# Rotary products summed on GpSimd before TensorE's transposes, and projections moved ahead of softmax steps

## The reference

```python
qkv = x @ qkv_w.T + qkv_b            # 32 query heads, 8 key heads, 8 value heads, 64 wide
q = _apply_rope(q, cos, sin)         # [x1*cos - x2*sin, x2*cos + x1*sin]
k = _apply_rope(k, cos, sin)
logits = einsum('bqhmd,bkhd->bhmqk', q, k) / 8      # causal, window 128
e = exp(logits - max);  w = e / (sum(e) + exp(sink - max))
out = einsum('bhmqk,bkhd->bqhmd', w, v) @ out_w.T + out_b
```

## Time and profile before

| what | us |
|---|---|
| median of three runs (2179.29, 2182.62, 2183.5) | 2182.62 |
| the profiled execution, its own time | 2175.44 |
| its span, from the first to the last instruction | 2173.4 |
| TensorE busy in the span | 1990.2 (92%) |
| VectorE busy | 1172.4 (54%) |
| ScalarE busy | 775.8 (36%) |
| GpSimd busy | 614.6 (28%) |

### The profile page before, as it was taken

One profiled execution on the slowest core, in us unless ns is written; L12 is line 12 of the kernel. 1 busy time (PEld: TensorE's weight loads), 2 busy tenths in 40 slices (PEclk: granted clock), 3 DMA queues, 4 the chain that ended last, 5 costly groups with the idle time before them and its releaser, 6 DMA issues. The chain is left out here.

```text
span 2173.4 us, 49370 instructions
## 1 busy us (share of the span) xinstructions
PE 1990.2 (92%) x17680; PEld 1484.0 (68%) x17681; DVE 1172.4 (54%) x2333; ACT 775.8 (36%) x1463; POOL 614.6 (28%) x1100
## 2 busy tenths in 40 slices
PE   4999999999999999997799999999999599999998
PEld 3877787778777877786566666666666355666665
DVE  6566556655665566555566566666666122222221
ACT  3333333333333333333245444445455211211211
POOL 2232223222322232222222333332332310014443
PEclk9999999999999999999799999999999799999999
DMA  4011111111111111111323323323222155222221
GB/s 160 26 50 37 48 36 48 36 48 36 48 36 48 36 48 36 48 33 52 94 57 81 83 59 81 79 63 81 74 68 66 39 173 185 70 66 66 66 64 43
DMA packets 123545, 139.65 MB, mean 64 GB/s; under 512 B 16706, under 2 KB 118086, under 8 KB 121642
## 3 DMA queue, kind: packets, MB, share of 16 engines
q1 hardware_dynamic: 117674, 123.95, 20.3%
q0 software_dynamic: 5760, 14.06, 2.0%
HBM read 85.07 MB, written 53.52 MB: 64 GB/s over the span
## 5 line engine op out<-in xcount | busy, mean ns | idle before, releaser
L1032 ACT ACTIVATE xe<-bankXT 128x512 f32<-128x512 f32 x512 | 289.2, 596 | 324.8 <-PE bankXT L1173 317.8
L1073 DVE TENSOR_REDUCE xmax<-bankX 128x4 f32<-128x1024 f32 x256 | 309.2, 1210 | 133.5 <-PE bankX L1162 133.5
L1162 PE MATMUL bankX<-stk,stq 96*128 96x256 f32 x1024 | 230.7, 311 | 24.0 <-DMA rw<-in_rw 10.2
L543 DVE TENSOR_TENSOR oTl<-bankV,oTh 128x512 fp32r<-128x512 f32 x128 | 88.5, 691 | 303.9 <-ACT oTh L431 303.9
L1173 PE MATMUL bankXT<-stq,stk 98*128 98x256 f32 x1024 | 220.5, 298 | 6.7 <-ACT xe L1032 2.8
L1162 PEld LDWEIGHTS bankX<-stk,stq 96*128 96x128 f32 x1024 | 162.3, 198 | 55.5 <-issue 32.0
L649 PE MATMUL bankQ<-wqh,xnTh 128*128 128x512 f32 x384 | 188.5, 491 | 0.0
L1472 DVE TENSOR_TENSOR hid<-bankU,gate 128x512 f32<-128x512 f32 x72 | 49.8, 691 | 245.0 <-PE bankU L1525 241.9
L1173 PEld LDWEIGHTS bankXT<-stq,stk 98*128 98x128 f32 x1024 | 157.4, 191 | 32.0 <-ACT xe L1032 27.6
L360 POOL TENSOR_TENSOR prob<-prob,rden 128x1024 f32<-128x1024 f32 x64 | 121.9, 1905 | 170.5 <-DVE rden L539 170.5
L1188 PE MATMUL bankN<-xe,cT 128*32 128x256 f32 x2048 | 166.2, 397 | 0.2 <-ACT xe L1032 0.2
(11 more groups left out here) (177 smaller groups left out, 4090.2 us busy)
## 6 DMA issues: line engine op xcount, KB each, us to landing
stackk_d<-chl SPq DMA_DIRECT2D x96, 128.0 KB, 2.3
stackq_d<-q2hl SPq DMA_DIRECT2D x96, 128.0 KB, 2.3
stk<-stackk_d SPq DMA_DIRECT2D x32, 384.0 KB
stq<-stackq_d SPq DMA_DIRECT2D x128, 96.0 KB
wexp<-in_wexp SPq DMA_DIRECT2D x8, 1536.0 KB, 8.5
x_d<-x SPq DMA_DIRECT2D x64, 128.0 KB, 2.0
xin<-xg_d SPq DMA_DIRECT2D x40, 128.5 KB, 2.1
x<-in_x SPq DMA_DIRECT2D x32, 128.0 KB, 2.2
```

Source lines behind the costliest of these rows:

```text
L543: nc.vector.tensor_tensor(oTl[g % 2][:], bV[:, 0, :].rearrange("p (a b) -> p a b", a=4), oTh[g % 2][:].bitcast(F32), ALU.subtract).then_in ...
L1032: nc.scalar.activation(xe[q % 8][:].rearrange("p n m -> p (n m)"), bT[:, q % 2, :], ACT.Exp).then_inc(s_xe, 1)
L1073: nc.vector.tensor_reduce(xmax[tile[1] % 2][:, :, a:b + 1:b - a].rearrange("p m h -> p h m"), bS[:, 2 * (pr % 2):2 * (pr % 2) + 2, :].rear ...
L1162: ins = nc.tensor.matmul(bS[:, q % 4, m * D:(m + 1) * D], stq[p][0:96, hd, m * P:(m + 1) * P], stk[p][0:96, hd // 4, :], start=True, stop= ...
```

## The change

The sum of the two rotary products is formed on GpSimd by a new helper, `rope_sum`, into three new buffers `roped[0..2]`. `turn_qk` then makes four transposes instead of eight. A new semaphore `s_rsum` counts the sums: `turn_qk(n)` waits for sum n, and `rope(c)` waits for sum c-2 (before: for the transposes of c-2). `rope_sum(c)` waits for `rope(c)` and, from c = 3 on, for the transposes that read the same one of the three buffers.

The order changes on all four engines. On TensorE, P2 stands ahead of Q0, P3 ahead of T0, P4 ahead of R0, P5 ahead of O1, and Q3 behind R2. On VectorE, `rope(2)` stands ahead of `shift(u, 1)`, `rope(3)` and `rest_O(u, 0)` ahead of `denominator(u, 1)`, and `rope(4)` right behind it. On ScalarE, `evac_PT(u, 0)` and `evac_qk(1)` stand ahead of `exp_probs(u, 1)`, and `evac_O(u, 2)` ahead of `evac_qk(3)`. On GpSimd the five sums are put between the existing steps, and `rsqrt(0)` moves ahead of the split of `q2`.

```diff
+        roped = [sb(f"roped{p}", [P, 512]) for p in range(3)]
...
+            def rope_sum(tile, c):
+
+                t = num(tile)
+                pool.wait_ge(s_rope, t * 5 + c + 1)
+                need(pool, s_turn, t * 5 + c - 2 if c >= 3 else t * 5)
+                nc.gpsimd.tensor_tensor(roped[c % 3][:], ropeC[c % 2][:], ropeD[c % 2][:], ALU.add).then_inc(s_rsum, 1)
...
                 dve.wait_ge(s_qkv, t * 6 + c + 1)
-                need(dve, s_turn, t * 5 + max(c - 1, 0))
+                need(dve, s_rsum, t * 5 + max(c - 1, 0))
...
-                pe.wait_ge(s_rope, t * 5 + n + 1)
+                pe.wait_ge(s_rsum, t * 5 + n + 1)
                 need(pe, s_qkT, t * 5 + n)
                 for j in range(4):
-                    for i, r in enumerate((ropeC[n % 2], ropeD[n % 2])):
-                        ins = turn(bT[:, 0, j * P:(j + 1) * P], r[:, j * P:(j + 1) * P], i == 0, i == 1)
+                    ins = turn(bT[:, 0, j * P:(j + 1) * P], roped[n % 3][:, j * P:(j + 1) * P])
...
                 if rear:
                     scores(u, 1)
                 if front:
+                    project(tile, 2)
                     turn_qk(tile, 0)
-                    project(tile, 2)
+                    project(tile, 3)
                 if rear:
                     turn_probs(u, 0)
                 if front:
                     turn_qk(tile, 1)
-                    project(tile, 3)
+                    project(tile, 4)
                 if rear:
                     results(u, 0)
                     turn_probs(u, 1)
                 if front:
                     turn_qk(tile, 2)
-                    project(tile, 4)
                 if rear:
                     project_out(u, 0)
                     results(u, 1)
                     turn_probs(u, 2)
                 if front:
-                    turn_qk(tile, 3)
+                    project(tile, 5)
                 if rear:
                     project_out(u, 1)
                     results(u, 2)
                 if front:
-                    project(tile, 5)
+                    turn_qk(tile, 3)
```

More of the change, by code:

```diff
@@ L205, in attention @@
         s_xnTp, s_xnTh, s_xnT = sem("s_xnTp"), sem("s_xnTh"), sem("s_xnT")
-        s_qkv, s_rope, s_v = sem("s_qkv"), sem("s_rope"), sem("s_v")
+        s_qkv, s_rope, s_v, s_rsum = sem("s_qkv"), sem("s_rope"), sem("s_v"), sem("s_rsum")
         s_turn, s_qkT = sem("s_turn"), sem("s_qkT")
@@ L367, in body @@
                     rsqrt(1, v)
+                if front:
+                    rope_sum(tile, 0)
                 if rear:
@@ L370, in body @@
                 if front:
+                    rope_sum(tile, 1)
+                    rope_sum(tile, 2)
                     pool.wait_ge(s_ctx[p], (h + 1) * 16)
                     split(tile, ctx[p][:], chl[p], s_stk[p], s_chl, g_c, 3)
+                    rope_sum(tile, 3)
                 if rear:
                     norm_probs(u, 1)
+                if front:
+                    rope_sum(tile, 4)
+                    if below(num(tile), NT - 2):
+                        rsqrt(0, (h + 1, p))
                 if prep:
@@ L377, in body @@
                     split(v, q2[:], q2hl[p], s_stq[p], s_q2hl, g_q2, 4)
-                if front:
-                    if below(num(tile), NT - 2):
-                        rsqrt(0, (h + 1, p))
             rsqrt(0, (0, 0))
@@ L443, in body @@
                 if rear:
-                    exp_probs(u, 1)
                     evac_PT(u, 0)
@@ L448, in body @@
                 if rear:
+                    exp_probs(u, 1)
                     evac_O(u, 0)
@@ L455, in body @@
                     evac_PT(u, 2)
+                    evac_O(u, 2)
                 if front:
@@ L458, in body @@
                 if rear:
-                    evac_O(u, 2)
                     evac_PT(u, 3)
@@ L585, in body @@
                     rope(tile, 1)
+                    rope(tile, 2)
                 if rear:
@@ L588, in body @@
                 if front:
-                    rope(tile, 2)
+                    rope(tile, 3)
                 if rear:
+                    rest_O(u, 0)
                     denominator(u, 1, soft)
-                    rest_O(u, 0)
                 if front:
-                    rope(tile, 3)
+                    rope(tile, 4)
                 if prep:
@@ L601, in body @@
                     stats1((h + 1, p))
-                if front:
-                    rope(tile, 4)
                 if rear:
```

## The result

| what | before | changed |
|---|---|---|
| median (runs; lowest to highest), us | 2183.06 (4; 2179.29 to 2185.14) | 2160.16 (4; 2151.27 to 2162.8) |
| changed / before, 95% interval | | 0.9896 [0.9875, 0.9917] |
| span of the profiled execution | 2173.4 | 2149.0 |
| mean of the two tiles laid out | 31.06 | 30.57 |
| last residual, the end of the self-attention | 1035.26 | 1019.68 |

The kernel became faster by 22.9 us, where 9 were forecast. The direction was right, and the forecast gain was less than half of what came. The 2160.16 lies inside the range of 2158 to 2187, but at its fast end: to anything faster than 2163 the prediction gave 0.07.

What follows compares the result with a forecast made beforehand. TensorE, busy 92%, sets the pace together with VectorE's chain to GpSimd's normalisation. Per tile 0.51 us saved less 0.18 for the sums, times 31, less about 1 us in the last tile: 9 us, so 2173.6; range 2158 to 2187.

Steps and rivals of the forecast that it cites:

- the two tiles laid out: Consecutive attention tiles from P0 at 511.33 and 542.56: 31.23 and 30.88 us, forecast 30.65 and 30.44 before the sums' cost.
- The gaps: Four new waits of TensorE in a tile, at P3, O0, T2 and O2: 1.0, 0.7, 1.3 and 0.7 us.
- The rival of a longer exclusion: VectorE kept out behind GpSimd's queue after the c = 2 sum: 30 us slower, 2213; all slower cases together 0.12.
- The dear and the cheap sum: Rivals on GpSimd's additions: 1.47 us, total 2186, within slower cases of 0.11; 1.12 us or less, 2163 to 2169, 0.25.
- the 15 us worked out from that page: Total saving if a GpSimd sum takes 1.12 us, in proportion to the skill's 4497 ns for 2048 wide.
- a gain of 0.33: Per attention tile: 0.51 us saved by the new layout less 0.18 lost to the sums on GpSimd.
- the 0.04: Loss per tile at Q1: its sum reaches TensorE at 10.48, TensorE is free at 10.43.
- 0.14: Time TensorE follows the end of GpSimd's normalisation, taken from T0 (520.44 to 520.58) and applied to T2.
- The sentence that closes the layout: Of 2.2 us saved in transposes and 1.6 of old gaps per tile, all but 0.51 goes into four new gaps.
- a loss of 1 us for the last tile: Last tile, without a front: denominator(1) stands behind rest_O(0), so about 1 us is lost.
- tile A: Attention tile beginning with P0 at 511.33, 31.23 us long; forecast to end at 30.65 before the sums' cost.

Runs made afterwards that it cites:

- experiment 10: Experiment 8 with R2 ahead of O1 on TensorE; 2097.85 us, ratio 0.9626 to the kernel before.
- Experiment 4: The changed kernel itself measured and profiled once more, nothing altered; 2158.24 us, ratio 0.9904 to the kernel before.
- experiment 7: Experiment 1 plus, on ScalarE alone, the copies of T0 and Q1 ahead of the exponential of half 1; 2155.31 us, ratio 0.9881 to the kernel before.
- experiment 5: The changed kernel with 36 extra unused matmuls on TensorE behind the last tile's output projection; 2160.91 us, ratio 0.9907 to the kernel before.
- experiment 8: Experiment 3 with each GpSimd normalisation split into two 512-wide halves, each with its own semaphore count; 2125.39 us, ratio 0.9739 to the kernel before.
- experiment 11: Experiment 10 with the second layer norm's statistics behind rope(2) and rsqrt(1) ahead of the sum of c = 3; 2079.71 us, ratio 0.9541 to the kernel before.
- 6: The kernel before with 36 extra unused matmuls on TensorE behind the last tile's output projection; 2181.98 us, ratio 1.0005 to the kernel before.
- 9: The changed kernel with 67 extra matmuls ahead of its first tile to delay its start; 2171.85 us, ratio 0.9969 to the kernel before.
- experiment 3: The changed kernel with the sum of c = 2 moved behind the split of ctx on GpSimd; 2150.24 us, ratio 0.9865 to the kernel before.
- experiment 1: The kernel before with only the sums put on GpSimd, the order on TensorE, VectorE and ScalarE kept; 2171.47 us, ratio 0.9963 to the kernel before.

## Why the prediction was right and wrong

**Right.** The places, releasers and most times of the tile, counted from P0. P3 at 8.39 (forecast 8.38), T0 without a gap, R0 at 12.51 (12.50). A sum took 1.29 us in the mean of 160 (1.27). `prob<-sinks,mx` began at 10.69 (10.70), took 0.93 and ended at 11.62 (11.60), right behind the sum of c = 2, which ended at 11.58. The exponential began at 12.78 (12.77), R0's copy at 13.76 (13.75). O2 came 2.44 after R2. The gaps were 0.88, 0.78, 0.97 and 0.54 for a forecast of 1.0, 0.7, 1.3 and 0.7. The rotary products weren't slowed (means 684 and 680 ns before, 681 and 679 after). The rival of a longer exclusion had no part: VectorE came in 0.04 after the sum although GpSimd had its small step queued behind it, and the longest of the 64 `prob<-sinks,mx` took 1.00 us. The dear and the cheap sum fall with 1.29.

The Trainium skill (GPSIMD Engine Reference, section 3.1) gives, in proportion, 1.12 us for such a sum. The trace doesn't agree: 1.29, so the 15 us worked out from that page had no ground, and that the time came out beyond even those 15 says nothing for it.

**Wrong 1: terms of the layout, 0.16 us a tile.** I gave a tile a gain of 0.33, and it was 0.49. Q1 didn't wait: the sum was there at 514.03 (10.43), when TensorE was free, so the 0.04 was nothing. From the end of the normalisation to T2 TensorE took 0.06 (522.26 to 522.32), not 0.14: 0.14 was the follow-on of T0 in the earlier trace rows, where other waits than this one may have stood, and I carried it over without a second row. P5 to O1 was the 1.61 laid out, but O1 to R2 1.40 and not 1.52 (the step of 1.52 was taken from an output projection that had stood in a wait). Two terms went the other way: T2, which had stood in a wait, took 0.49 and not 0.44 (as T0 did in the earlier trace rows, 520.58 to 521.07), and O2 to the end 6.01 and not 5.98. That is 0.04 + 0.08 + 0.12 - 0.05 - 0.03 = 0.16; times 31 it is 5 us, more than half of what I forecast.

The sentence that closes the layout doesn't add up either: 2.2 saved and 1.6 of old gaps, less new gaps of 3.7, leave 0.1 and not 0.51. I had read the old gaps as idle time from their rows and laid the new ones out from start to start, where a gap is longer (experiment 10). The starts, which carry the sum, don't have this slip.

**Wrong 2: the ends of the stage.** I laid out the middle and took a loss of 1 us for the last tile, because the second denominator stands behind R0's rest there. It gained. TensorE in the last tile, with S1 and then T0, R0 and the first output projection, before:

```profile
1010.36 0.60 PE L670 MATMUL bankS<-maskb,identb 128*128 128x512 bf16 x2 [3.09 <-DVE prob L530]
...
1018.08 2.08 PE L701 MATMUL bankV<-probT,vbd 128*128 128x256 f32 x4 [1.77 <-ACT probT L425]
```

and changed:

```profile
995.20 0.60 PE L682 MATMUL bankS<-maskb,identb 128*128 128x512 bf16 x2 [3.09 <-DVE prob L544]
...
1001.38 2.07 PE L713 MATMUL bankV<-probT,vbd 128*128 128x256 f32 x4 [0.69 <-ACT probT L439]
```

From S1 to R0 it was 7.72 and is 6.18, because ScalarE copies T0's result ahead of the exponential. From S1 to the last residual only 0.4 of these 1.5 us is left (24.90 before, 24.48 now). The other 1.1 isn't the late denominator but the clock. The first output projection of this tile, stretch view, before and changed:

```profile
1021.57:1023.10 1.53, 1.53 (x13) 1.53 (x14) 0.27 (x1) 0.07 (x1) 1.11 (x2) 1.00 0.05 11
```

```profile
1004.87:1007.52 2.65, 2.65 (x13) 2.65 (x14) 1.73 (x4) 0.07 (x1) 1.01 (x1) 0.53 0.00 0
```

TensorE had stood for 3.09 and 3.14 us ahead of this in the changed kernel, for 3.09, 2.32 and 1.77 in the one before. The same thirteen matmuls then ran at 0.53, near the 1.2 GHz level, in the changed one. Experiment 4 shows the same tile without this: its first output projection took 1.61 us (from 1004.26, at a granted clock of 0.94), and from S1 (995.12) to the last residual (1018.01) it was 22.9, 2.0 less than before, of which 1.95 lie ahead of R0. T2 did wait 0.98 us there for the late normalisation, and it cost nothing: R1's rest was ready only when T2 was done, and from R1 to the last residual it took 12.14 us, as before (12.16). So the step that failed is the loss of 1 us: I priced the late denominator by itself and not against the wait that ends last. I had listed ScalarE's edit in the change and given it no term, and by experiment 7 it is the one edit of the order that the tile needed. The first residual also comes 1.2 us earlier. From the first to the last residual it is 957.7 before and 943.3 after, 14.4 us, plus 1.2: the 15.6 of the table, against 9 forecast.

**Wrong 3: the sum's frame.** I made the saving of one stage the saving of the program. The stages behind the attention took 1138.1 and 1137.5 us in two profiles of the kernel before, 1129.3 and 1134.3 in two of the changed kernel, and between 1129.3 and 1146.5 over all kernels here. So 3 to 9 us of the gain lie there, some 5 to 7 in the medians. No part of the change stands there. It goes with the granted clock: over eight runs of the changed kernel (those of experiment 4 among them), span and mean clock are 2159.9 at 0.976, 2159.2 at 0.977 (three runs), 2154.0 at 0.980 (three) and 2149.0 at 0.981. That is the whole program; the stretch views show where. The next stage runs at 1.00 but for short pieces at 0.50, some 3.4 us each, seven in the kernel before and five in the changed one; in the ten microseconds ahead of those that I viewed TensorE had worked 6.5 to 8.8. One of them, kernel before:

```profile
1116.90:1120.10 3.20, 3.20 (x28) 1.72 (x31) 2.14 (x5) 1.43 (x4) 1.88 (x6) 0.50 0.08 21
```

From the first to the last layer-norm statistics this stage took 617.6 to 618.2 us in the three profiles that had 20 to 23 us of it at half clock, 620 to 625 in the nine that had 25 to 33, and 629.5 in the two that had 36 to 40. These fourteen are all the profiles here, and they don't stand in the order in which the attention ended: experiment 5, with the changed attention, has 624.0, experiment 8, whose attention ends 50 us before that of the kernel before, 624.7, and experiment 11 620.3. So the length goes with the time at half clock, some 0.7 us for each us. Why one kernel meets more of it than another is open; keeping TensorE busy ahead of the stage (5, 6) and a later start (9) did not settle it. My range treated this stretch as fixed, while two profiles of the changed kernel alone differ by 5 us in it.

In sum, with the first profiles' figures: 9 forecast; 5 for the terms of the layout (31 x 0.16); 1 to 2 for the ends; 7 in stages not touched. That makes 22 to 23 of 22.9, where the 7 is the remainder and so closes the sum by itself. The terms of the layout and the ends are shown by rows; the last is located, and tied to the clock, but not explained.

## What to carry to other kernels

When work moves from the busiest engine to an idle one, lay out the new waits start by start, and price every edit of the order, those on the engines that seem to have time too: here two lines of ScalarE decided whether halved transposes gave 9 us or 26. A gap on the pacing engine that ends with one long instruction elsewhere is worth splitting that instruction, even if the parts cost more together (experiment 8). And when a sum of a few terms of 0.1 us is multiplied by 31 tiles, each term needs a row of its own kind (a step behind a wait and one without a wait are not the same kind), and the range needs the scatter of the stages that the change doesn't touch.

## What the runs showed of the hardware

VectorE is shut out by a running GpSimd instruction also with an operation of one input and per-partition scalars. The normalise of the layer norm, over the attention, in the changed kernel:

```profile
L503 DVE TENSOR_SCALAR q<-x,mv,rstd 128x256 f32<-128x256 f32 x32 | 30.8, 963 | 1.4 <-POOL rstd L341 1.4
```

In the kernel before it took 403 ns. In tile A it ended at 522.41, GpSimd's normalisation at 522.26. I had given it no term, and no wait of TensorE on VectorE follows it there. The Trainium skill (SBUF — State Buffer, Who interferes with whom) names this kind of operation among those that can take the shared pair of ports; the trace agrees, with 0.99 against 0.40.

A block of VectorE costs only what the next engine's queue makes of it: some 0.75 us of it cost 0.156 us a tile in the changed kernel, where R0's copy stood behind the exponential (experiment 3). In experiment 1, where T0's copy did, TensorE stood 0.67 us, and taking the copy out from behind the exponential gave 0.46 us a tile (experiment 7); what of that is the block's was not tested by itself. And one kernel's execution can move by 11 us of 2155 with a mean granted clock between 0.976 and 0.981, more than the whole gain that I had forecast.
